# Norm deviations formed on TensorE, a two-part maximum, a rewritten order of the steady loop, and unread matrix products, in a 16-sample attention, expert and memory kernel

## The reference

```python
h = _layernorm(x) * (1 + ca) + sa                # norm 1
x = x + ga * attn(h)                             # 16 heads of 8, softmax over 256 keys
h = _layernorm(x) * (1 + cb) + sb                # norm 2
x = x + gb * experts(h)                          # 16 experts, top 4 of 16, clipped gate and up
h = _layernorm(x) * (1 + ca) + sa                # norm 3
v, k = h @ Wv, exp(1j * 10 * h @ Wk)             # 16 heads of 64
mem = cumsum(v * rotor) , cumsum(v * conj(k_shifted))
x = x + ga * (real(mem * probe) / sqrt(t) * gates) @ Wo
h = _layernorm(x) * (1 + cb) + sb                # norm 4
x = x + gb * sigmoid(xr @ W_r) * (relu(xk @ W_k) ** 2 @ W_v)   # xr, xk mix h with its shift by one token
```

## Time and profile before

| | |
|---|---|
| median of 3 runs | 1406.51 us (1405.9 to 1409.64) |
| profiled execution | 1408.67 us, of which the span of the trace 1406.9 us |
| mean granted TensorE clock | 0.975 of full speed |
| busy, TensorE / VectorE / ScalarE / GpSimd | 1208.3 / 1157.6 / 968.0 / 282.7 us |

### The profile page before, as it was taken

One profiled execution on the slowest core, in us unless ns is written; L12 is line 12 of the kernel. 1 busy time (PEld: TensorE's weight loads), 2 busy tenths in 40 slices (PEclk: granted clock), 3 DMA queues, 4 the chain that ended last, 5 costly groups with the idle time before them and its releaser, 6 DMA issues.

```text
span 1406.9 us, 22222 instructions
## 1 busy us (share of the span) xinstructions
PE 1208.3 (86%) x6866; PEld 904.8 (64%) x6866; DVE 1157.6 (82%) x2151; ACT 968.0 (69%) x1698; POOL 282.7 (20%) x260
## 2 busy tenths in 40 slices
PE   6788898989889898988989898898989889898987
PEld 5465675857667585756758576675857567585765
DVE  7758979797987979798797979879797987979765
ACT  1565767778676777867677786767778676776841
POOL 4221131303112130311313031121303112130200
PEclk9789999999999999999999999999999999999997
DMA  6340210303030020303003030301203030120000
GB/s 125 92 38 1 27 16 10 27 8 34 8 27 14 10 23 8 34 8 30 12 9 25 8 34 8 29 12 11 22 8 34 8 30 12 11 23 5 1 4 4
DMA packets 54663, 29.94 MB, mean 21 GB/s; under 512 B 3741, under 2 KB 53610, under 8 KB 54634
## 3 DMA queue, kind: packets, MB, share of 16 engines
q1 hardware_dynamic: 52744, 28.87, 16.8%
q10 hardware_dynamic: 1890, 0.70, 0.5%
HBM read 8.20 MB, written 2.10 MB: 7 GB/s over the span
## 4 chain that ended last, share of the span: by engine, by line
PE 53%; DVE 17%; ACT 15%; issue 11%; POOL 2%; ACTq 1%; DMA 1%; DVEq 0%; POOLq 0%
PE ring L752 16%; PE pa L766 7%; PE pb L852 6%; DVE smax L1783 5%; PE pa L686 4%; PE ring L673 3%; ACT prob L1259 2%; PE ring L739 2%; DVE prod L1901 2%; PE pb_k L782 2%; PE ring L635 2%; ACT L1357 1%; ACT frac L1360 1%; ACT sin_t L1357 1%; DVE prod L1896 1%
## 5 line engine op out<-in xcount | busy, mean ns | idle before, releaser
L433 POOL TENSOR_TENSOR gsc<-gsc,sc_all 128x512 f32<-128x512 f32 x128 | 169.1, 1326 | 370.4 <-ACT gsc L1318 370.4
L752 PE MATMUL ring<-ht,wgu 128*128 128x256 f32 x1024 | 242.4, 385 | 0.5 <-ACT sc_all L1306 0.5
L1928 DVE TENSOR_TENSOR_SCAN prod<-keep,prod 128x512 f32<-128x512 f32 x188 | 223.8, 1211 | 0.0
L752 PEld LDWEIGHTS ring<-ht,wgu 128*128 128x128 f32 x1024 | 193.8, 192 | 34.9 <-issue 5.0
L1783 DVE TENSOR_REDUCE smax<-ring 128x4 f32<-128x1024 f32 x128 | 153.3, 1218 | 14.8 <-PE ring L635 9.5
L852 PE MATMUL pb<-prod,wo 128*128 128x256 f32 x544 | 129.9, 383 | 17.9 <-DVE prod L1942 17.9
L1861 DVE SCALAR_TENSOR_TENSOR prob<-prob,gsc 128x512 f32<-128x512 f32 x120 | 81.4, 688 | 68.8 <-POOL gsc L433 64.1
L1259 ACT ACTIVATE prob<-ring 128x1024 f32<-128x1024 f32 x128 | 125.7, 1024 | 11.4 <-PE ring L673 9.8
L1313 ACT ACTIVATE gsc<-ring,gub_t 128x256 f32<-128x256 f32 x256 | 110.6, 501 | 24.6 <-PE ring L752 24.5
L852 PEld LDWEIGHTS pb<-prod,wo 128*128 128x128 f32 x544 | 102.6, 191 | 34.0 <-DVE prod L1942 20.6
L766 PE MATMUL pa<-prob,wdown 128*128 128x256 f32 x512 | 122.9, 382 | 1.8 <-DVE prob L1855 1.8
(11 more groups left out here) (283 smaller groups left out, 2412.7 us busy)
## 6 DMA issues: line engine op xcount, KB each, us to landing
q_rows<-qk_part SPq DMA_DIRECT2D x144, 64.0 KB
k_rows<-qk_part SPq DMA_DIRECT2D x135, 64.0 KB
x_in<-in_L_attn_x_dram SPq DMA_DIRECT2D x16, 128.0 KB, 2.1
sc_all<-_L_ffn_gate_up_proj_dram SPq DMA_DIRECT2D x1, 2048.0 KB, 12.1
out_dram<-xo SPq DMA_DIRECT2D x16, 128.0 KB, 1.8
prob<-in_L_wmod_dram SPq DMA_DIRECT2D x2, 384.0 KB, 5.2
k_rows<-qk_part ACTq DMA_DIRECT2D x9, 64.0 KB
...
```

The lines of the kernel that those rows point to most:

```text
L433: pool.tensor_tensor(gsc[:, n % NG, :], gsc[:, n % NG, :], sca, ALU.mult).then_inc(S["gsc"], 1)
L752: last = mm(ring[:, n % 2, g * 512 + j * L:g * 512 + (j + 1) * L], lhsT=wgu[:, 2 * n + j, g, :], rhs=ht[:, :], start=True, stop=True, skip ...
L1928: nc.vector.tensor_tensor_scan(prod[:, h, n - 1, :], keep[:, :], prod[:, h, n - 1, :], 0.0, ALU.mult, ALU.add).then_inc(S["cu" + str(n)], 1)
```

## The change

**Norms 2 to 4.** The matrix of the first product becomes ident - 1/128 (`cent_w`), so TensorE's product is x less its mean. VectorE's subtraction is gone; ScalarE copies the product out of PSUM (new event `dev`) and then squares the copy. `scale` also waits for `dev`.

**Maximum.** `split_max` makes two bf16 parts in two operations instead of three parts in five; `m_sb` and the DMA have 32 rows instead of 48, and the scores use 126 rows instead of 125.

**First sample.** ScalarE instead of GpSimd copies the expert weights into `wgu`, before the first `exps` instead of beside them. The absolute value of the rotor angles moves from ScalarE to VectorE. On ScalarE `part` and `part_2` of sample 1 go behind the four `copy_broadcast`, and `down_scaled` goes between the halves of norm 2. On TensorE `attn_out_1` and `attn_out_2` go ahead of `turn_rotors` 1 to 3.

**Unread products.** `warm(n, bank)` issues n fp32 products (ident times `upper`, 256 columns) into a bank whose content nobody reads: 10 at the start of `first` and 6 ahead of its `turn_scores`; in every step 2 before `memory_wo(b, 1)` and 3 (`WARM`) in `broadcast(0)` ahead of the wait for `sctb` (in `first` too); in the last step 4, 4 and 2 more; in `last` 28 around norm 4 and the last sub-layer.

**Steady order.** All three lists of `step` are written anew, and `last` follows. The first products of the next memory layer move to the end of the step. The new lists (a, b, x stand for the sample; p = phases, pv = phase_values, tv = time_values, st = scores_t, v = values, wo = memory_wo, gu = gate_up, dp = down_pair, sc = scores, bc = broadcast; on VectorE A, P, B, C, O, D, S12, S = memory_a ... memory_s, with block and part):

The diff, cut to its core (the lists above stand for the `step` hunks):

```diff
+mean_w = sb("mean_w", [P, 1])
+cent_w = sb("cent_w", [P, P])
...
-    need(pool, "s_ps", 0, ST)
-    pool.wait_ge(*upto("dve", "ffn_v"))
-    pool.tensor_copy(wgu[:, :, 0, :], sc_all[:, :, 0:L:2]).then_inc(*mark("pool", "wgu_g"))
-    pool.tensor_copy(wgu[:, :, 1, :], sc_all[:, :, 1:L:2]).then_inc(*mark("pool", "wgu_u"))
...
-def mean(b, n, src, src_sem, ps, free):
+def centre(b, n, src, src_sem, ps, free):
...
-    mm(ps[:, 0:L], lhsT=mean_w[:, :], rhs=src, start=True, stop=True,
-       skip_group_check=True).then_inc(S["mean" + n], 1)
+    mm(ps[:, 0:L], lhsT=cent_w[:, :], rhs=src, start=True, stop=True,
+       skip_group_check=True).then_inc(S["cent" + n], 1)
...
-    need(pe, "mp2", b, 1)
+    need(pe, "mp1", b, 1)
     for n in range(NT):
-        last = tr(ring[0:3 * H, 0, :].bitcast(BF16)[:, n * P:(n + 1) * P],
+        last = tr(ring[0:2 * H, 0, :].bitcast(BF16)[:, n * P:(n + 1) * P],
...
+def warm(n, bank):
+    for _ in range(n):
+        mm(bank[:, 0:L], lhsT=ident[:, :], rhs=upper[:, :], start=True, stop=True, skip_group_check=True)
+
+def warm_last(nx, n):
+    if nx is None:
+        warm(n, ring[:, 0, :])
+
+def warm_scores(b, n):
+    need(pe, "ya", b, 1)
+    warm(n, ring[:, 1, :])
+
 def turn_scores(b):
+    need(pe, "ya", b, 1)
     need(pe, "sp2", b, 1)
     need(pe, "sc", b, 1)
-    need(pe, "ya", b, 1)
...
     if n == 0:
-        need(pe, "sctb", b, 1)
         need(pe, "lg", b, 1)
         if nx is not None:
             need(pe, "q_sb", nx, 1)
             need(pe, "k_sb", nx, 1)
+        warm(WARM, ring[:, 0, :])
+        need(pe, "sctb", b, 1)
...
+    upper_made()
+    warm(10, pb_k)
     turn_max(a)
...
-    mean(b, "4", x3[:, :], "x3", pb, ())
+    warm(4, ring[:, 0, :])
+    centre(b, "4", x3[:, :], "x3", pb, ())
+    warm(4, ring[:, 0, :])
     variance(b, "4", pb, sqb)
+    warm(4, ring[:, 0, :])
     deviation(b, "4", pb, rstdb)
+    warm(8, ring[:, 0, :])
     mix_1(b)
+    warm(4, ring[:, 0, :])
     mix_2(b)
+    warm(4, ring[:, 0, :])
     mix_3(b)
...
+def square(b, n, ps, c, s):
     need(act, "cent" + n, b, 1)
+    other, same = {"2": ("h2", 0), "3": ("h4", 0), "4": ("h3", 1)}[n]
+    need(act, other, b, same)
+    if n == "3":
+        need(act, "xk", b, 0)
+    af(c[:, :], ps[:, 0:L], ACT.Copy).then_inc(S["dev" + n], 1)
+    need(act, "dev" + n, b, 1)
     af(s[:, :], c[:, :], ACT.Square).then_inc(S["sq" + n], 1)

...
+def expert_weights(b):
+    act.wait_ge(SET["ld_gu"], 16)
+    need(act, "s_ps", b, ST)
+    af(wgu[:, :, 0, :], sc_all[:, :, 0:L:2], ACT.Copy).then_inc(*mark("act", "wgu_g"))
+    af(wgu[:, :, 1, :], sc_all[:, :, 1:L:2], ACT.Copy).then_inc(*mark("act", "wgu_u"))
...
     copy_max(a)
+    expert_weights(a)
     exps(a, 0)
...
+    dve.wait_ge(*upto("pool", "ident"))
+    ts(cent_w[:, :], ident[:, :], 1.0 / D, None, ALU.subtract)
...
+def angles_abs():
+    ang = prod[:, 0, :, :].rearrange("p a b -> p (a b)")
+    tmp = prod[:, 1, :, :].rearrange("p a b -> p (a b)")
+    stt(out=tmp, in0=ang, scalar=-1.0, in1=ang, op0=ALU.mult, op1=ALU.max).then_inc(*mark("dve", "ang_abs"))
...
-def centre(b, n, src, dst, ps):
...
-    need(dve, other, b, same)
-    tt(dst[:, :], src[:, :], ps[:, 0:L], ALU.subtract).then_inc(S["cent" + n], 1)
-
...
 def scale(b, n, c, ps):
     need(dve, "rbc" + n, b, 1)
+    need(dve, "dev" + n, b, 1)
...

 def split_max(b):
     need(dve, "s_max", b, ST)
-    ts(negm[:, :, :], smax[:, :, :], -1.0, None, ALU.mult).then_inc(S["neg"], 1)
-    need(dve, "neg", b, 1)
-    nc.vector.tensor_copy(mpart[:, :, 0, :], negm[:, :, :]).then_inc(S["mp0"], 1)
+    ts(mpart[:, :, 0, :], smax[:, :, :], -1.0, None, ALU.mult).then_inc(S["mp0"], 1)
     need(dve, "mp0", b, 1)
-    tt(mrest[:, :, :], negm[:, :, :], mpart[:, :, 0, :], ALU.subtract).then_inc(S["mr0"], 1)
-    need(dve, "mr0", b, 1)
-    nc.vector.tensor_copy(mpart[:, :, 1, :], mrest[:, :, :]).then_inc(S["mp1"], 1)
-    need(dve, "mp1", b, 1)
-    tt(mpart[:, :, 2, :], mrest[:, :, :], mpart[:, :, 1, :], ALU.subtract).then_inc(S["mp2"], 1)
+    stt(out=mpart[:, :, 1, :], in0=smax[:, :, :], scalar=-1.0, in1=mpart[:, :, 0, :], op0=ALU.mult,
+        op1=ALU.subtract).then_inc(S["mp1"], 1)

```

More of the change, by code:

```diff
@@ L949, in step @@
                 if on_b:
-                    memory_wo(b, 0)
+                    phase_values(b, 2)
+                if on_x:
+                    head_1(nx)
+                if on_a:
+                    centre(a, "2", x1[:, :], "x1", pa, ())
+                if on_b:
+                    time_values(b, 2)
                 if on_x:
@@ L1402, in step @@
                 if on_b:
-                    phase(b, 0)
-                    value(b, 0)
                     tables(b, 0)
@@ L1440, in step @@
                 if on_x:
-                    part(nx)
-                if on_a:
-                    second_norm_2(a)
-                if on_x:
-                    part_2(nx)
-                if on_b:
-                    value(b, 3)
-                if on_a:
-                    route(a)
+                    head_2(nx)
                 if on_b:
@@ L1452, in step @@
                 if on_a:
+                    second_norm_2(a)
+                if on_b:
+                    value(b, 3)
+                if on_x:
+                    part(nx)
+                if on_a:
+                    route(a)
                     copy_scores(a)
@@ L1502, in step @@
                     mix_2(b)
+                if on_a:
+                    phase(a, 0)
+                    value(a, 0)
             def first(a, nx):
                 copy_max(a)
+                expert_weights(a)
                 exps(a, 0)
@@ L1534, in first @@
                 copy_broadcast(a, 3)
+                part(nx)
+                part_2(nx)
                 gate_clip(a, 0)
@@ L1550, in first @@
                 bend(a, 7)
-                square(a, "3", centb, sqb)
+                square(a, "3", pb, centb, sqb)
                 modulate(a, "3", centb, hb[:, 1:L + 1], mod_b, 6)
+                phase(a, 0)
+                value(a, 0)
             def last(b):
-                phase(b, 0)
-                value(b, 0)
                 phase(b, 1)
@@ L2099, in step @@
                 if on_b:
-                    memory_s12(b, 3)
-                    memory_end(b)
+                    epsilon(b, "4", vepsb, pb)
                 if on_a:
@@ L2123, in step @@
                 if on_a:
-                    centre3(a)
+                    experts_out(a)
+                if on_b:
+                    mix_in(b)
                 if on_x:
@@ L2134, in step @@
                 if on_a:
-                    scale(a, "3", centb, pb)
                     next_b(a)
+                if on_x:
+                    maxima(nx, 5)
+                    maxima(nx, 6)
+                if on_a:
+                    memory_a(a, 0)
             def first(a, nx):
```

345 lines of the change are left out of this document (159 added, 186 removed).

## The result

The changed kernel takes **1445.72 us** (median of 4 runs, 1441.73 to 1455.94) where the kernel before took 1406.2 beside it: ratio 1.030, 95% interval 1.027 to 1.033. It is slower by 3%; the forecast was 1368.

The account below looks back on a forecast made before the run. No engine alone bounds: handovers and VectorE's queue in the front, TensorE's products in the experts. First sample -10, steps -21, clock -2, end -5.5 make -38.5; with 2.2 off for the median, 1408.67 becomes 1368 us, range 1346 to 1396.

Parts of the forecast that it names:

- The step that failed: `part_2`: ScalarE ahead of the last two broadcasts: `part_2` counted as 0.6 us, within the +0.55 from `turn_scores` to first `gate_up`.
- The step's own sum: Steady step: -1.85 + 0.55 - 0.1 - 0.1 = -1.5 us, 14 times that -21; bounds nothing and -2.6 a step.
- The front: From `maxima` 7 to `turn_scores`: shorter VectorE queue and latency chain, 35.7 us against 37.55, so -1.85.
- The experts: First `gate_up` to last `down_pair`: `down_bias` gone (-0.6), third `gate_up` waits 0.5, net -0.1 us a step.
- the rear: From x2 to the next `maxima` 7: 10.4 us where it was 10.55, so -0.1 a step.
- The arithmetic: Maximum and norms 2 to 4: VectorE gains 0.6 us on the maximum and 0.4 on each norm's subtraction.
- The clock: Steady steps' pauses: unread products there keep TensorE's clock up, -2 us for all steps, bound 0.
- Unread products: Two ahead of `memory_wo(b, 1)` cost nothing unless its pause goes; rival: all five on TensorE's path, +1.35 a step, chance 0.07.
- First sample: First sample: ScalarE's copies instead of GpSimd's and new order, -10 us, between -7 and -13; first `gate_up` 9 earlier.
- the lock on VectorE: First sample: VectorE's angle operations, run beside GpSimd's copies, get back 1.7 + 1.86 = 3.6 us.
- End: Last step and `last`: step gain 1.5, clock, and new order of `last` at -3; -5.5 us, between -2 and -8.
- The rival of the other sign: Experts: ScalarE waits for norm 4's product, delayed by scans beside GpSimd; 5 us a step gives 1424 us; chance 0.10.

Follow-up runs that it names:

- e1: The changed kernel with ScalarE's `part_2` of the steady step moved forward, right behind `route`: 1421.9 us, ratio to before 1.011.
- e7: e1 with ScalarE's order at the start of the experts as before the change (`gate_clip` 0 and 2 earlier): 1416.8 us, ratio 1.006.
- e4: The kernel before with only the new arithmetic (norms 2 to 4, two-part maximum), every list in its old order: 1409.2 us, ratio 1.002.
- e3: e1 without the five unread products of a steady step: 1449.7 us, ratio to before 1.029.
- e8: e1 with `split_max` directly behind `maxima` 7 on VectorE, as in the kernel before: 1422.5 us, ratio to before 1.012.
- e12: e7 with two unread products for three ahead of the broadcasts and `down_bias` behind the third `gate_up`: 1422.0 us, ratio to before 1.010.
- e5: e4 with four unread products a steady step, two ahead of `memory_wo(b, 1)` and two ahead of the broadcasts: 1398.3 us, ratio 0.993.
- e6: e5 with most of the change's first-sample edits and eleven unread products in `last`, which keeps its old order: 1390.9 us, ratio 0.989.

## Why the prediction was wrong

TensorE's timeline of one undisturbed step of before (its maxima's DMA starts at 373.38) and of e1 (at 376.58): the first transpose of the scores, the first experts, the first scores of the next sample.

```profile
407.56 0.39 PE L722 MATMUL ring<-ident,sc 128*16 128x128 f32 x2
413.59 3.72 PE L752 MATMUL ring<-ht,wgu 128*128 128x256 f32 x16
...
437.27 1.03 PE L635 MATMUL ring<-k_rows,q_rows 125*128 125x256 bf16 x8 [0.21 <-ACT prob L1324]
```

```profile
409.24 0.38 PE L732 MATMUL ring<-ident,sc 128*16 128x128 f32 x2
416.10 3.72 PE L763 MATMUL ring<-ht,wgu 128*128 128x256 f32 x16 [0.68 <-ACT sc_all L1336]
420.58 1.99 PE L763 MATMUL ring<-ht,wgu 128*128 128x256 f32 x8 [0.76 <-ACT gsc L1343]
...
440.91 1.03 PE L630 MATMUL ring<-k_rows,q_rows 126*128 126x256 bf16 x8 [0.19 <-ACT prob L1354]
```

Counted as in the prediction from the start of `maxima` 7 (370.00 and 372.55) to the next one, with the time in which TensorE is idle:

| | before | e1 | change | forecast | TensorE idle, before and e1 |
|---|---|---|---|---|---|
| to `turn_scores` | 37.56 | 36.69 | -0.87 | -1.85 | 7.1, 5.2 |
| to the first `gate_up` | 6.03 | 6.86 | +0.83 | +0.55 | 1.2, 0.7 |
| to `scores(nx, 0)` | 23.68 | 24.81 | +1.13 | -0.1 | 0.2, 1.0 |
| to the next `maxima` 7 | 14.39 | 14.61 | +0.22 | -0.1 | 1.7, 2.6 |
| step | 81.66 | 82.97 | +1.31 | -1.5 | 10.3, 9.5 |

TensorE works 2.1 us more in e1's step, the width of the five unread products (2.15), and its idle time is only 0.8 shorter.

*The step that failed: `part_2`.* The prediction put it at 0.6 us of ScalarE ahead of the last broadcast, and stopped there. It issues nothing itself, but GpSimd's last subtraction waits for it, SyncE's queue for that, and 1.18 MB in 18 transfers behind that, 24 us long. Between their landing and `scores` there were about 9 us before; the move took 11. No rival held it. It accounts for 24 of the 39 us by the medians (33 of 47 by the profiles).

*The step's own sum* failed too, and the sign with it: +1.3 with the rows early. The front was right in kind and half in size, 0.87 of 1.85: TensorE's idle time there fell by 1.85, but the two products ahead of `memory_wo(b, 1)`, which I had at nothing, are in it. The experts are where it broke. I had -0.1 for them and took a third `gate_up` wait of 0.5 as paid by `down_bias`; the wait is 0.76, and e7 shows that it makes 0.5 of the step's length. One more `down_pair` (0.86 us) also stands ahead of `scores(nx, 0)` than before, so the rear has that much less to do and is still 0.22 longer: TensorE waits 0.9 more there, in several short handovers. Of the +1.3, the arithmetic is -0.45 (e4 against before at clock 1.00), the five products are +0.45 (e3's one step at 1.00), and ScalarE's order at the start of the experts is +0.5 (e7). The remaining 0.8 have no cause that a run has shown: the wait of `turn_max` is not it (e8), and `down_bias` behind the third `gate_up` with a product fewer doesn't give it back (e12).

*The arithmetic.* VectorE's saving is there, 0.45 us a step (e4 against before at clock 1.00), and worth nothing by itself, as the clock fell in six of the fourteen steps (two before).

*The clock* was sized at 2 us for the whole kernel, from before alone. In the changed kernel's profile it is 6.4 us of loss, where I had 2 of gain, and with another filling of the pauses it is worth far more: 28 us between e1 and e3, about 11 between e4 and e5. Removing work around a pause can lengthen the pause and bring the clock down where it had held.

*Unread products.* In the old order four cost nothing (e5). In the new one five cost 0.45 us a step, which I had as a rival at 0.07 and with 1.35, and are needed. At the end 28 cost 2.3 to 3.6 us over 11, where I had them even with the clock.

*First sample.* Forecast -10, measured -1.9. ScalarE's copies and the lock on VectorE came as said: the copies take 2.1 us each, three operations of VectorE of 128x2048 in a row take 6.94, 2.3 each, where before the two beside GpSimd's copies took 3.98 and 4.14. The router's product came 4.4 us sooner and the first `gate_up` 5.9 (81.13), where I had 9. In e6 the sample keeps 6.7 us of gain, just under my range, and e5 shows that 3.2 of them are not the ends'. The changed kernel lost it again between the first `gate_up` and the maxima, with the late rows (scores at 109.55 after 2.79 us idle, and at half clock: 1.89 us for 1.04 in e6), and with the ten products ahead of `turn_max`, which run for 4.4 us:

```profile
33.78 4.48 PE L717 MATMUL pb_k<-upper,ident 128*128 128x256 f32 x20
38.19 0.29 PE L653 MATMUL ring<-identb,mpart 128*32 128x128 bf16 x2
```

*End.* Forecast -5.5, measured -0.4 in the changed kernel; e6, with fewer products, in the old order of `last`, gets -5.3, and e4, with the arithmetic alone, -3.7 (clock 0.94 in the stretch for 0.89). The new order of `last` was not tried by itself.

*The rival of the other sign* (ScalarE in the experts) did not come: ScalarE stands idle for 0.49 us ahead of its copy for norm 4 (e1, 435.18; the same in the changed kernel). One `expert_last` a step is longer beside GpSimd, 1.67 us for 0.69 (e1, 428.18), and ScalarE waits 0.36 for it. The rival gave the right direction by a wrong mechanism, so its 0.10 was luck.
